# A graph network's second layer as straight-line programs with rings of four quads, its guard found by powers of four, and attention's loops unrolled

## The reference

```python
h = relu(layernorm(x)); x = x + mean layer:  (segment_sum(h[src], dst) / count) @ W_l.T + b_l + h @ W_r.T
h = relu(layernorm(x)); x = x + relation layer: segment_sum over edge_dst=dst of w[:, b] * h[src] for 2 bases, then a matrix product
h = relu(layernorm(x)); x = x + attention over row=src, col=dst:
    alpha = sum_c q[row] * (k[col] + edge_attr @ We) / sqrt(32)          # 4 heads of 32
    m = zeros((n, H)).at[row].set(alpha)                                 # one edge of each source node
    ex = exp(alpha - m[row]);  out = segment_sum(v[col] * ex / segment_sum(ex)[row], row), then a gate with the skip product
h = relu(layernorm(x)); x = x + segment_sum(h[dst], src)
```

## Time and profile before

| | us |
|---|---|
| median of 3 runs (15730.9 to 15737.61) | 15736.96 |
| profiled execution, its own time | 15853.16 |
| its span, first to last instruction | 15851.3 |
| instructions in the span | 127777 |

### The profile page before, as it was taken

The page is one execution under the profiler, slowest core; times in us unless marked ns, Lnnn a source line. Parts: engine busy times, 40 slices in busy tenths (PEclk is TensorE's granted clock), DMA queues, the critical chain, the costliest instruction groups (busy, mean ns, idle before and its releaser), DMA issues. The chain is left out here.

```text
span 15851.3 us, 127777 instructions
## 1 busy us (share of the span) xinstructions
PE 5342.2 (34%) x26456; PEld 4326.3 (27%) x26457; DVE 5110.9 (32%) x13143; ACT 2948.8 (19%) x8860; POOL 9554.7 (60%) x9670
## 2 busy tenths in 40 slices
PE   3111102333331000005455555545555553333333
PEld 1000002233331000003333333445545453222322
DVE  5111102222221000004444444545555545222222
ACT  0000000000000000005555555323333331000000
POOL 3777776666666777765455455255555553666665
PEclk7555555555555555557767777777777776555555
DMA  1000001111111010001111111122222222222222
GB/s 63 10 2 2 2 2 37 46 46 46 46 46 23 13 21 13 13 16 41 41 41 41 41 41 41 28 85 80 79 81 80 81 78 57 51 50 51 51 51 55
DMA packets 649313, 668.90 MB, mean 42 GB/s; under 512 B 419156, under 2 KB 515576, under 8 KB 648360
## 3 DMA queue, kind: packets, MB, share of 16 engines
q0 software_dynamic: 335184, 555.05, 14.3%
q1 hardware_dynamic: 313944, 111.86, 3.1%
HBM read 609.46 MB, written 56.70 MB: 42 GB/s over the span
## 5 line engine op out<-in xcount | busy, mean ns | idle before, releaser
L523 POOL DMA_INDIRECT l_rows<-h_tab,l_words x3232 | 3099.6, 959 | 1879.7 <-issue 953.9
L565 PE MATMUL l_sums<-l_rows,l_onehot 128*128 128x129 f32 (+1 forms) x6464 | 1662.5, 438 | 3769.4 <-issue 2074.8
L565 PEld LDWEIGHTS l_sums<-l_rows,l_onehot 128*128 128x128 f32 x6464 | 1443.4, 328 | 3988.8 <-issue 2859.2
L756 POOL DMA_INDIRECT l_rows<-h_tab,l_words_d x1616 | 1527.6, 945 | 1525.4 <-ACT l_msg L784 1016.6
L1168 POOL DMA_INDIRECT l_kv<-kv_tab,l_words x1616 | 1555.6, 963 | 1304.9 <-DMA l_words<-by_src 605.0
L113 POOL DMA_INDIRECT by_dst<-words,rows x1564 | 1665.8, 1065 | 758.0 <-issue 521.3
L553 DVE TENSOR_TENSOR acc<-acc,l_sums 128x129 f32 (+1 forms) x3232 | 931.0, 288 | 3450.6 <-remote 1203.3
L113 POOL DMA_INDIRECT by_src<-l0n_words,l0n_rows x1564 | 1650.9, 1056 | 535.2 <-issue 519.8
L1297 PE MATMUL l_ps_q<-qtab,h 128*128 x3232 | 881.1, 432 | 1227.5 <-ACT h L1190 751.7
L874 PE MATMUL l_rank<-l_onehot_s,before 128*128 128x128 bf16 x1616 | 244.3, 306 | 2898.3 <-issue 1602.6
L900 PE MATMUL l_sums<-l_msg,l_onehot 128*128 128x256 f32 x3232 | 1188.4, 532 | 31.2 <-ACT l_msg L784 18.1
(11 more groups left out here) (225 smaller groups left out, 7442.2 us busy)
## 6 DMA issues: line engine op xcount, KB each, us to landing
l_rows<-h_tab,l_words POOLq DMA_INDIRECT x3232
l_words<-by_src SPq DMA_DIRECT2D x808, 38.0 KB
l_rows<-h_tab,l_words_d POOLq DMA_INDIRECT x1616
l_kv<-kv_tab,l_words POOLq DMA_INDIRECT x1616
by_dst<-words,rows POOLq DMA_INDIRECT x1564
by_src<-l0n_words,l0n_rows POOLq DMA_INDIRECT x1564
l_words_s<-by_src SPq DMA_DIRECT2D x202, 76.0 KB
by_src<-h SPq DMA_DIRECT2D x4, 3136.0 KB, 27.7
```

Of the source, the lines that this page charges most:

```text
L523: pool.indirect_dma_start(rows[b][:, j, 0:D], None, table, bass.IndirectOffsetOnAxis(ap=words[b][:, j, 0:1], axis=0)).then_inc(rows_ready[ ...
L565: done = nc.tensor.matmul(sums[b][:, j, 0:cols], onehot[b][:, j, :], rows[b][:, j, :], start=True, stop=True)
L756: pool.indirect_dma_start(rows[s][:, j, :], None, h_tab, bass.IndirectOffsetOnAxis(ap=words_d[s][:, j, 0:1], axis=0)).then_inc(rows_ready[ ...
```

## The change

- The second layer's stage is written out for 404 quads, with four buffers of words, rows, messages and one-hots, and two of sums. VectorE makes both one-hots (L471's helper) two quads ahead; ScalarE only scales.
- The guard: a product of the tile's source one-hot with two columns of powers of four (`lane`: 64 edges each, 4 to the power of the place) gives, per node, a sum whose exponent tells the last edge. VectorE shifts the exponent out once in four quads, adds the tile's number times 512 and keeps the maximum per node in `code`. At the end 14 operations turn `code` into row numbers of `by_src`.
- `project_phase` gathers these 49 x 128 rows of `by_src` into `rep` beside its first half. Attention reads the destination from there.
- `by_src` has 18 words, without the destination as a float; one copy per round in `mean_phase`, one conversion in the sort and its table go; the sort makes `lane` (memset, two iotas, one copy).
- Attention's loops of SyncE, GpSimd and, in `steps_of`, of ScalarE, VectorE and TensorE become Python loops.

```diff
-WS = 3 + ED
+WS = 2 + ED
+CODE = 512
@@ sort_phase
+                ch.link(nc.gpsimd.memset(lane_bits[:], 0))
+                for half in range(2):
+                    ch.link(nc.gpsimd.iota(lane_bits[64 * half:64 * half + 64, half:half + 1], pattern=[[0, 1]],
+                                           base=63 << 23, channel_multiplier=1 << 24))
-                nc.vector.tensor_copy(dstf[:], dst_i[:])
+                nc.vector.tensor_copy(lane[:], lane_bits[:].bitcast(F32))
@@ mean_phase
-                    nc.scalar.activation(wf[:, s, :, 1:2], dstf[:, bass.ds(at, SC)].unsqueeze(2), ACT.Copy)
@@ relation_phase, now
+    H, RING, AHEAD = G // 2, 4, 2
+    QUADS, T4 = TILES // H, RING * H
+            @block.sync
+                for q in range(QUADS):
+                    b, half = q % RING, q % 2
+                    if q >= RING:
+                        sp.wait_ge(scaled, q - RING + 1)
+                        sp.wait_ge(oh_ready, q - RING + 1)
+                    sp.dma_start(words_d[b] ...).then_inc(dready[b], 16)
+                    if q >= RING:
+                        sp.wait_ge(ohs_ready, q - RING + 1)
+                    sp.dma_start(words_s[b] ...).then_inc(sready[b], 16)
+            @block.gpsimd
+                for q in range(QUADS):
+                    if q >= RING:
+                        pool.wait_ge(scaled, q - RING + 1)
+                    pool.wait_ge(dready[b], 16 * (q // RING + 1))
...
+            @block.scalar
+                for q in range(QUADS):
+                    if q >= RING:
+                        act.wait_ge(summed, pairs_of(q - RING))
+                    act.wait_ge(rows_ready[b], 16 * H * (q // RING + 1))
...
+            @block.vector
+                def one_hots(q):
+                    s = q % RING
+                    if q >= RING:
+                        dve.wait_ge(summed, pairs_of(q - RING))
+                    dve.wait_ge(dready[s], 16 * (q // RING + 1))
+                    one_hot(nc, onehot[s][:], place, words_d[s][:].bitcast(F32)[:, :, 1:2], H).then_inc(oh_ready, 1)
+                    if q >= RING:
+                        dve.wait_ge(picked, q - RING + 1)
+                    dve.wait_ge(sready[s], 16 * (q // RING + 1))
+                    one_hot(nc, onehot_s[s][:], minus, words_s[s][:].bitcast(F32)[:, :, 1:2], H).then_inc(ohs_ready, 1)
...
+                def keep_edges(r):
+                    dve.wait_ge(picked, (r + 1) * RING)
+                    nc.vector.tensor_scalar(power[:], pick[:, :, 0:2].bitcast(I32), 23, None, ALU.logical_shift_right).then_inc(decoded, 1)
+                    dve.wait_ge(decoded, r + 1)
+                    own_links.link(nc.vector.scalar_tensor_tensor(mark[:], power[:, :, 1:2], 2.0, power[:, :, 0:1], ALU.mult, ALU.max))
+                    own_links.link(nc.vector.scalar_tensor_tensor(found[:], mark[:], 0.0, tile_no[:, r * T4:(r + 1) * T4, :], ALU.is_gt, ALU.mult))
+                    own_links.link(nc.vector.tensor_tensor(found[:], found[:], mark[:], ALU.add))
+                    for half in range(2):
+                        blocks = blocks_of(nc, ENGINE.DVE, blk_src, r * T4 + half * G, G)
+                        for j in range(G):
+                            dve.wait_ge(kept, r * T4 + half * G + j + 1)
+                            c = code[:, bass.ds(blocks[j], 1), :]
+                            nc.vector.tensor_tensor(c, c, found[:, half * G + j:half * G + j + 1, :], ALU.max).then_inc(kept, 1)
...
+                for q in range(QUADS):
+                    if q + AHEAD < QUADS:
+                        one_hots(q + AHEAD)
+                    add_up(q)
+                    if q % RING == RING - 1:
+                        keep_edges(q // RING)
+            @block.tensor
+                for q in range(QUADS):
+                    b = q % RING
+                    if b == 0 and q:
+                        pe.wait_ge(decoded, q // RING)
+                    pe.wait_ge(ohs_ready, q + 1)
+                    for j in range(H):
+                        last = nc.tensor.matmul(pick[:, b * H + j, 0:2], onehot_s[b][:, j, :], lane[:], start=True, stop=True)
+                    last.then_inc(picked, 1)
+                    pe.wait_ge(scaled, q + 1)
+                    for j in range(H):
+                        if j % 2 == 0 and q >= 2:
+                            pe.wait_ge(added, (q - 2) * H + j + 2)
+                        done = nc.tensor.matmul(sums[q % 2][:, j, :], onehot[b][:, j, :], msg[b][:, j, :], start=True, stop=True)
+                        if j % 2 == 1:
+                            done.then_inc(summed, 1)
@@ project_phase, first half
+                    @block.gpsimd
+                    def _(pool):
+                        for b in range(NB):
+                            pool.indirect_dma_start(rep[:, b, :], None, by_src, bass.IndirectOffsetOnAxis(ap=rep_row[:, b, :], axis=0)
+                                                    ).then_inc(rep_loaded, 16)
+                        pool.wait_ge(rep_loaded, 16 * NB)
@@ attend_phase
-            with eng.Fori(0, rounds) as i:
+            for i in range(rounds):
-                with sp.Fori(1, ITERS) as i:
+                for i in range(1, ITERS):
-                with pool.Fori(1, ITERS) as i:
+                for i in range(1, ITERS):
```

More of the change, by code:

```diff
@@ L878, in picks @@
-                def picks(i, s):
-                    for j in range(G):
-                        if j % H == 0:
-                            pe.wait_ge(firsts, i * 4 + (2 * s + j // H + 1))
-                        if j == 0:
-                            pe.wait_ge(split, i * 4 + (2 * s + 3))
-                            pe.wait_ge(kept, i * T2 + (s * G + G))
-                        parts = (words_s[s % 2][:].bitcast(F32)[:, j, 1:WS], rest[0][:, j, :], rest[1][:, j, :])
-                        for n, w in enumerate(parts):
-                            last = nc.tensor.matmul(pick[s % 2][:, j, 0:WS - 1], first[:, j, :], upper(w), start=(n == 0), stop=(n == 2))
-                    last.then_inc(picked, 1)
@@ L891, in step @@
-                def step(i, s, last=False):
-                    for j in range(G):
-                        if j == H and not last:
-                            ranks(i, s + 1)
-                        if j % H == 0:
-                            pe.wait_ge(oh_ready, i * 4 + (2 * s + j // H + 5))
-                        if j % 2 == 0:
-                            pe.wait_ge(added, i * T2 + (s * G + j + 2 + G))
-                        pe.wait_ge(scaled, i * T2 + (s * G + j + 1 + T2))
-                        nc.tensor.matmul(sums[:, j, :], onehot[s][:, j, :], msg[s][:, j, :], start=True, stop=True).then_inc(summed, 1)
-                    if not last:
-                        picks(i, s + 1)
@@ L1199, in one_hots @@
                     for e in range(Q):
[L1200 removed]
+                        last = nc.scalar.activation(apart[q][:, e, :], place[:], ACT.Abs, bias=words[s][:].bitcast(F32)[:, q * Q + e, 1:2])
                     last.then_inc(apart_ready, 1)
```

264 lines of the change are left out of this document (95 added, 169 removed).

## The result

The change takes 15223.26 us, median of 4 runs (15210.57 to 15233.38), the kernel before 15733.93 (15700.38 to 15737.61, 4 runs). The ratio is 0.968, 95% interval 0.9663 to 0.9696: 511 us, 3.2%, faster. The profiled execution took 15226.07 us. Forecast were 15145, and 15262 for the profiled execution.

The account below looks back on a forecast made before the run. The prediction took the kernel as bound by waits, no engine being busy over 60%. It summed 15853.2 - 561 + 5 + 15 - 50 = 15262 us profiled, and 116 less gave 15145, range 14780 to 15600.

Parts of the forecast that it names:

- Second layer, 2508 + 5: Second layer: 2120 us of VectorE's work plus 388 exposed lateness, 561 less than 3068.6; 5 us more for decoding the guard.
- 97 late completions at 4 us exposed: Second layer: one late completion per 100 TensorE records, 6.5 us each, 4 of it exposed, 388 us in all.
- Rival B: Second layer: rings and double-buffered sums cover the late completions; stage near 2150 us, kernel 14790; chance 0.20.
- The path of GpSimd: Second layer: gathers wait only for scaling four quads back, so GpSimd runs eight quads (40 us) ahead; floor 2020 us.
- GpSimd waiting for ScalarE's scaling ... not for words: Second layer, expected sign: GpSimd waits for scaling because the ring is full, not for edge words.
- VectorE busy near 60% and above GpSimd: Second layer, expected sign: VectorE busy near 60% of the stage, above GpSimd's 50% or more.
- VectorE's terms: Second layer: one-hots 1.37, adds 2.36 and guard 1.55 us per quad, 5.28 together; 21.0 us per round of four.
- Projection, +15: Projection, 216.8 us before: 49 added gathers, 61 us of work mostly hidden, cost 15 us; bounds 0 and 61.
- Attention, -50: Attention: unrolling saves 0.1 us per quad, 40, and 10 for 100 turns; ends -200 and +50.
- The 116 us between profile and median: Whole kernel: the median of runs stands 116 us under the profiled time, subtracted to forecast 15145 us.
- Rival E: Second layer: VectorE operations with two SBUF inputs lengthen gathers; 7.04 us per quad, stage 2844 us, kernel 15480; chance 0.05.
- no, and I keep 1.25 us: Second layer: a busier VectorE does not slow GpSimd's gathers, which keep starting every 1.25 us.

Follow-up runs that it names:

- e8: The change with the second layer's 1616 gathers left out and fixed rows loaded plainly instead, on a late chip: 14668.9 us, before 15727.89.
- e10: The change with second-layer rings of six quads, three quads of sums and two buffers of picks, on a late chip: 15414.48 us, ratio 0.973.
- e7: The change with the by-destination one-hot on ScalarE again, in the same rings, on a late chip: 15397.35 us, ratio 0.9737.
- e9: The change with attention's hardware loops as before the change, on a late chip: 15319.57 us, ratio 0.9745.
- e2: The change with attention's hardware loops as before the change, on a prompt chip: 13048.42 us, ratio 1.0055.
- e6: The change with 37 of the projection's 49 gathers moved behind the first half's seven products, on a late chip: 15324.89 us, ratio 0.9687.
- e12: The change with second-layer rings of three quads and 37 of the projection's gathers moved later, on a prompt chip: 13091.8 us, ratio 1.0091.

## Why the prediction came right, and which terms were wrong

The forecast of the profiled execution, 15262, missed 15226 by 36 us. So close a hit is luck: the 36 are the sum of terms that were further off, in both directions: second layer +90, projection +21, attention -101, the sum stages -44, the rest -2.

- **Second layer, 2508 + 5: 2602.5, 90 too low.** The size was near, the reason was not. "97 late completions at 4 us exposed" on top of VectorE's 2120 fails: there are no isolated events to be counted per record. A round of VectorE takes 19.9 us, 2010 in all, and without gathers the stage takes 2023.9; the other 579 us come with the gathers (e8). Rival B, "covered", rested on the same price; the stage's 2602.6 us and e10 exclude it.
- **The path of GpSimd.** "A gather of quad q waits only for the scaling of quad q-4 ... so GpSimd can run eight quads ahead" left out the edge words. Their buffer is free only when VectorE has made the one-hot of quad q-4, and 117 of 123 stops ended that way. The sign "GpSimd waiting for ScalarE's scaling ... not for words" came out the other way round, and so did "VectorE busy near 60% and above GpSimd": VectorE is busy for 57%, GpSimd for 61% of the stage.
- **VectorE's terms held.** Maxima 0.165 us, 0.29 apart (0.17 and 0.31 forecast), a round 19.9 us (21.0). Whether a shorter round would help is open: GpSimd's own 5.0 us per quad is equal, and e7 moved work to ScalarE at the same time.
- **Projection, +15: +36.** I named the effect ("they can also make some of the first part's TensorE completions late") but priced it by a late completion's 6.5 us. The hold lasts as long as the string of gathers does.
- **Attention, -50: -151 between the profiles.** 80.5 is the unrolling, as e8 against e9 has it. The rest lies in the difference between two executions of late stages: the sum stages, unedited, moved by -21 and -23, and the same unrolled attention took 2785 to 2875 us in seven profiles on late chips.
- **The 116 us between profile and median** were no constant. The profile of the change sits 3 us from its median, and on the chip of e10 the kernel before has a median of 15844, so 116 us is what late chips differ by. Subtracting them was wrong: without that step the forecast is 39 us high, with it 78 low.
- **Rival E, the longer gathers,** holds in a small part, and "no, and I keep 1.25 us" was a wrong reading. What counts is the order in time. A gather that starts while a VectorE operation with two SBUF inputs runs is not done until 0.82 us after that operation's end; one that started before the operation takes its usual 0.945 us. Rows of e2's second layer, of the change's first sum stage, and of e6's projection:

```profile
6998.52 0.94 POOL L767 DMA_INDIRECT l_rows<-h_tab,l_words_d  x1 [0.30 <-issue]
6998.77 0.68 DVE L480 TENSOR_TENSOR l_onehot<-place,l_words_d 128x512 f32<-128x512 f32 x1
...
6999.37 0.68 DVE L480 TENSOR_TENSOR l_onehot_s<-minus,l_words_s 128x512 bf16<-128x512 f32 x1
6999.77 1.11 POOL L767 DMA_INDIRECT l_rows<-h_tab,l_words_d  x1 [0.30 <-issue]
```
```profile
2542.58 0.68 DVE L480 TENSOR_TENSOR l_onehot<-place,l_words 128x512 f32<-128x512 f32 x1
2542.72 1.37 POOL L532 DMA_INDIRECT l_rows<-h_tab,l_words  x1 [0.31 <-issue]
```
```profile
9765.96 6.69 DVE L63 TENSOR_TENSOR h<-x,stat 128x6272 f32<-128x6272 f32 x1
9766.74 6.73 POOL L939 DMA_INDIRECT guard_edge<-by_src,guard_row  x1 [0.30 <-issue]
...
9779.41 6.69 DVE L65 TENSOR_REDUCE stat<-tmp 128x49 f32<-128x6272 f32 x1
9780.50 0.94 POOL L939 DMA_INDIRECT guard_edge<-by_src,guard_row  x1 [0.30 <-issue]
```

One-hots with f32 and with bf16 results both do it; the reduction, which has one input, does not. In the change's second layer 255 of the 1616 gathers started while a one-hot had at least 0.1 us to run. They took 1.14 us on average, 50 us more in all; the rest took 0.945, but for one of 12.2 us. These are the 62 us by which the gathers got longer, where rival E had 336. In the kernel before no gather of the second layer met a one-hot so, and 83 of 3232 in the sum stages did: the three mean lengths of the prediction could not show the effect. The Trainium skill ("SBUF — State Buffer", section SBUF: two separate sides) states a lock between a VectorE operation with two SBUF inputs and a GpSimd operation that reads SBUF; whichever starts first keeps the shared ports for its whole length. A gather takes its row numbers from SBUF, and where VectorE starts first the rows agree.

That the change would be faster was right for the kind of chip that the profile of before came from, and only there. Nothing in that profile showed that its largest cost, GpSimd's and VectorE's waits ended by "remote", belonged to the chip and not to the program. What makes a chip late stays open.

## What to carry to other kernels

When a program's waits are ended by "remote" again and again, look at what GpSimd does meanwhile, and at whether another chip shows the same, before pricing them. Keep long strings of indirect transfers away from short hand-offs between other engines: 49 gathers in a row held one TensorE completion for 39 us. Moving them can cost time on a prompt chip (e12: 36 us). Ask of every buffer in a ring which engine releases it: here GpSimd's gathers hung on VectorE through the edge words, which the prediction had overlooked. And a ring that lets the issuing engine run further ahead does not help when its issuing is what holds the answers back.

## What the hardware showed unexpectedly

- The same program takes 12975 us on some chips and 15700 to 15850 on others, and each repeats its own time within 0.4% while it is measured. The first sum stage of the kernel before takes 2046.6 and 2431.5 us.
- On the late kind, waits for TensorE's updates end late in stages with GpSimd's indirect transfers, one by 39 us; without the gathers the second layer's stage takes 2023.9 us on both kinds.
- Pauses of 276 us in GpSimd's 1616 gathers cost nothing there.
- A gather that starts while a VectorE operation with two SBUF inputs runs ends 0.82 us after that operation, so it can take 6.7 us for 0.94; one that starts first is not lengthened.
